# Moving dense-expert steps ahead of a recurrence, and splitting a run of exponentials, in a two-layer transformer kernel

## The reference

```
# x: [8, 512, 128]; xn = layernorm(x)
mixed = silu(causal_dwconv(zrms(xn) @ W_qkvz[:, :2048]))   # 16 blocks of 128 channels, 4 taps
q, k, v = split(mixed)                                     # 4 + 4 + 8 heads of 128; q and k normalised
g, beta = -exp(A_log) * softplus(a + dt_bias), sigmoid(b)  # per token and head
for t in tokens:                                           # the recurrence ("gated delta rule")
    S = S * exp(g[t]); delta = (v[t] - k[t] @ S) * beta[t]
    S = S + outer(k[t], delta); o[t] = q[t] @ S
core = rms(o) * gate_norm_w * silu(z);  h = xn + core @ W_out
attn = h + moe(zrms(h))                                    # 8 small experts, top 2
# the dense experts, on the same xn: every token goes through all 8
w = top2(softmax(xn @ w_router))                           # [tokens, 8], zero but for two
ffn = sum_e w[:, e] * (gelu(xn @ w1[e] + b1[e]) @ w2[e] + b2[e])     # 512 hidden channels each
x = x + attn + ffn
```

## Time and profile before

| | us |
|---|---|
| median of 3 runs | 2765.76 |
| lowest, highest | 2764.23, 2774.04 |
| the profiled execution | 2770.14 |
| its span, first to last instruction | 2768.3 |
| TensorE busy in it | 2453.1 (89%) |
| VectorE busy | 2028.8 (73%) |
| ScalarE busy | 1136.2 (41%) |
| GpSimd busy | 311.6 (11%) |

### The profile page before, as it was taken

How to read it: one execution, slowest core, us unless ns; L and a number is a source line. 1 busy time by engine, 2 the same in 40 slices (tenths; PEclk the granted TensorE clock), 3 DMA queues, 4 the chain that set the end, 5 groups by cost and what they waited for, 6 DMA issues and landing times.

```text
span 2768.3 us, 48745 instructions
## 1 busy us (share of the span) xinstructions
PE 2453.1 (89%) x15408; PEld 1596.9 (58%) x15408; DVE 2028.8 (73%) x6361; ACT 1136.2 (41%) x2066; POOL 311.6 (11%) x236
## 2 busy tenths in 40 slices
PE   2989888898989887899899899899899899899898
PEld 1434344443444444586586586586586586577576
DVE  4857676685867777768777867867867966966976
ACT  0132322313232234446446445445445445544544
POOL 1000000000000001121121110210210211211211
PEclk8988889898988987999999999999899999899999
DMA  5230413212130312201201201101101101211210
GB/s 157 78 93 24 108 37 88 55 62 72 46 103 25 105 43 66 69 5 58 70 4 59 62 9 62 54 17 62 47 25 62 47 25 36 66 32 32 62 39 31
DMA packets 158271, 152.01 MB, mean 55 GB/s; under 512 B 81128, under 2 KB 122672, under 8 KB 157520
## 3 DMA queue, kind: packets, MB, share of 16 engines
q1 hardware_dynamic: 155024, 142.83, 18.0%
q10 hardware_dynamic: 3008, 6.36, 0.6%
HBM read 121.29 MB, written 27.85 MB: 54 GB/s over the span
## 4 chain that ended last, share of the span: by engine, by line
PE 56%; DVE 25%; issue 12%; ACT 3%; DMA 2%; POOL 1%; SPq 1%; DVEq 0%; ACTq 0%; POOLq 0%
PE bank L910 5%; PE bank L922 5%; PE bank L580 4%; PE bank L592 4%; PE bank L583 4%; PE bank L608 3%; PE bank L502 3%; DVE arena L1605 3%; DVE arena L1663 3%; DVE arena L1661 3%; PE bank L648 3%; PE bank L897 2%; PE bank L879 2%; DVE arena L1617 2%; PE bank L870 2%
## 5 line engine op out<-in xcount | busy, mean ns | idle before, releaser
L922 PEld LDWEIGHTS bank<-wring,arena 128*128 128x128 f32 x2048 | 279.9, 202 | 136.4 <-issue 99.0
L1166 ACT ACTIVATE arena<-bank,w_b 128x512 f32<-128x512 f32 x256 | 175.1, 687 | 369.6 <-PE bank L910 369.3
L910 PE MATMUL bank<-arena,wring 128*128 128x512 f32 x512 | 295.0, 662 | 30.9 <-ACT arena L1166 30.9
L922 PE MATMUL bank<-wring,arena 128*128 128x128 f32 x2048 | 284.7, 287 | 22.8 <-DVE arena L1778 15.2
L1605 DVE SCALAR_TENSOR_TENSOR arena<-bank,w_convw,arena 128x511 f32<-128x511 f32 (+2 forms) x384 | 254.9, 737 | 11.6 <-ACT arena L1076 11.6
L1045 ACT ACTIVATE arena<-bank 128x512 f32<-128x512 f32 (+1 forms) x384 | 172.5, 534 | 186.9 <-PE bank L635 185.3
L1449 DVE CUSTOM_DVE_ANT_0 bank<-bank,arena 128x128 f32<-128x128 f32 (+3 forms) x512 | 249.2, 492 | 0.0
L1036 ACT ACTIVATE arena<-bank 128x512 f32<-128x512 f32 x128 | 76.5, 598 | 397.4 <-PE bank L580 397.4
L502 PE MATMUL bank<-w_ident,arena 128*128 128x128 f32 (+2 forms) x652 | 114.9, 303 | 84.5 <-DVE arena L1345 51.9
L592 PE MATMUL bank<-arena 128*128 128x128 f32 x1088 | 157.5, 288 | 2.7 <-DVE arena L1434 2.7
L580 PE MATMUL bank<-arena 128*128 128x512 f32 x256 | 148.7, 664 | 0.0
(11 more groups left out here) (284 smaller groups left out, 4845.8 us busy)
## 6 DMA issues: line engine op xcount, KB each, us to landing
wring<-in_w_last SPq DMA_DIRECT2D x66, 512.0 KB, 3.3
arena<-scrw SPq DMA_DIRECT2D x260, 128.0 KB, 3.0
arena<-scrg SPq DMA_DIRECT2D x32, 512.0 KB, 5.4
arena<-scrq SPq DMA_DIRECT2D x36, 192.0 KB, 3.8
arena<-scrk SPq DMA_DIRECT2D x36, 192.0 KB, 4.5
scrn<-arena SPq DMA_DIRECT2D x64, 64.0 KB, 1.9
arena<-scrn SPq DMA_DIRECT2D x8, 512.0 KB, 3.7
scrx<-arena SPq DMA_DIRECT2D x8, 512.0 KB, 3.5
```

Of the source, the lines that this page charges most:

```text
L910: mm(bank[HBANK[f]][:, :], wring[:, e % 2, k * P:(k + 1) * P], xn1T, start=True, stop=True).then_inc(*s["p_fh"].up)
L922: last = mm(bank[o][:, t * P:(t + 1) * P], GH[:, f % 2, t * P:(t + 1) * P], wring[:, e % 2, FC * P + k * D:FC * P + (k + 1) * D], start=(f ...
L1166: fn(GH[:, f % 2, :], bank[HBANK[f]][:, :], ACT.Gelu_apprx_tanh, bias=W["b1"][:, f:f + 1]).then_inc(*s["a_gh"].up)
```

## The change

The order of the steps is altered, and with it the banks. The decay step `gam` is split: four exponentials, then the copies of `qkv 10` and `gelu 2`, then the other four; `prep 1`, `prep 2` and `prep 3` come one dense step later each. `fh 8` goes to bank 1 like `fh 0` and stands ahead of `qkv 12`; `fh 9` and `fo 8` come ahead of `sub 0`. Twenty-four dense steps are now finished before the recurrence (22 before), and eight follow it (10 before). Each expert is one part in one bank, so there are eight `facc`. The first three experts are summed in bank 6, one after the other. `facc 1` is moved from between `sub 1` and `sub 2` to between `taps 12` and `taps 14`. The waits follow the banks.

```
-HBANK = (1,) + (7,) * 21 + (2,) * 10
-PARTS = ((0, 4, 6), (4, 8, 6), (8, 12, 2), (12, 16, 3), (16, 20, 6), (20, 22, 6), (22, 24, 3), (24, 28, 5), (28, 32, 3))
+HBANK = (1,) + (7,) * 7 + (1,) + (7,) * 15 + (2,) * 8
+OBANK = (6, 6, 6, 3, 2, 6, 5, 3)
...
-    order += [("fo", 5), ("gelu", 6), ("fh", 7), ("fo", 6), ("gelu", 7), ("taps", 10), ("silu", 8), ("qkv", 12), ("fo", 7), ("taps", 12)]
+    order += [("fo", 5), ("fh", 7), ("gelu", 7), ("fh", 8), ("fo", 6), ("gelu", 8), ("taps", 10), ("silu", 8), ("qkv", 12), ("fo", 7)]
+    order += [("taps", 12), ("facc", 1), ("silu", 10), ("qkv", 14), ("taps", 14), ("cz", 0), ("silu", 12), ("sz", 0), ("fh", 9), ("fo", 8), ("cz", 1)]
...
-    order += ffn(2) + [("nrm2", NT - 1, 0), ("nrm2", NT - 1, 1)] + ffn(1) + [("ct", NT - 1), ("facc", 6)] + ffn(1) + [("swo", NT - 1), ("h1",)] + ffn(3)
+    order += ffn(1) + [("nrm2", NT - 1, 0), ("nrm2", NT - 1, 1)] + ffn(1) + [("ct", NT - 1)] + ffn(1) + [("swo", NT - 1), ("h1",)] + ffn(2)
...
                 def cz(c):
+                    if c == 0:
+                        need("a_gh", 9)
...
-                        need(*(("a_inv", a0) if c else ("v_fo", 16)))
+                        need(*(("a_inv", a0) if c else ("v_fo", 20)))
...
                     if f == 1:
                         pe.wait_ge(*s["out_ready"].at(b, 0, late))
-                    elif f == 22:
+                    elif f == 24:
                         need("v_inv", INV_V * NT)
+                    elif f == 8:
+                        need("v_prep", 2 * NT)
                     elif f:
-                        need("a_gh", f)
+                        need("a_gh", f - (f == 9))
...
-                    if f == first and f:
-                        need(*(("v_fo", 4), ("a_sz", 3), ("a_sz", 4), ("v_fo", 8), ("v_fo", 20), ("v_inv", INV_V * NT), ("v_o", 2 * NT),
-                               ("v_fo", 28))[part - 1])
+                    if k == 0 and e:
+                        need(*(("v_fo", 4), ("v_fo", 8), ("a_sz", 4), ("a_sz", 3), ("v_fo", 12), ("v_o", 2 * NT),
+                               ("v_inv", INV_V * NT))[e - 1])
...
-                def gam():
-                    act.wait_ge(*s["v_gT"].at(b, 1, late))
-                    fn(eG.rearrange("p a b c -> p (a b c)"), bank[0][:, 0:96], ACT.Exp).then_inc(*s["a_eG"].up)
-                    for i in range(2 * NT):
+                def gam(half):
+                    if half == 0:
+                        act.wait_ge(*s["v_gT"].at(b, 1, late))
+                        fn(eG.rearrange("p a b c -> p (a b c)"), bank[0][:, 0:96], ACT.Exp).then_inc(*s["a_eG"].up)
+                    for i in range(NT * half, NT * half + NT):
                         act.wait_ge(*s["v_scan"].at(b, i + 1, late))
                         fn(Gam[:, i, :], Gam[:, i, :], ACT.Exp).then_inc(*s["a_gam"].up)
```

More of the change, by code:

```diff
@@ L846, in kt @@
                     if c < NT - 1:
[L847 removed]
+                        bk = after(*(("a_gh", 24), ("v_kd", 2), ("a_ct", 2))[c], 7)
                         for h in range(HK):
@@ L914, in ffn_out @@
                     e, k = f // FC, f % FC
-                    part = [f < end for _, end, _ in PARTS].index(True)
-                    first, end, o = PARTS[part]
                     pe.wait_ge(*s["a_gh"].at(b, f + 1, late))
-                    if f == first and f:
-                        need(*(("v_fo", 4), ("a_sz", 3), ("a_sz", 4), ("v_fo", 8), ("v_fo", 20), ("v_inv", INV_V * NT), ("v_o", 2 * NT),
-                               ("v_fo", 28))[part - 1])
+                    if k == 0 and e:
+                        need(*(("v_fo", 4), ("v_fo", 8), ("a_sz", 4), ("a_sz", 3), ("v_fo", 12), ("v_o", 2 * NT),
+                               ("v_inv", INV_V * NT))[e - 1])
                     for t in range(NT):
-                        last = mm(bank[o][:, t * P:(t + 1) * P], GH[:, f % 2, t * P:(t + 1) * P],
+                        last = mm(bank[OBANK[e]][:, t * P:(t + 1) * P], GH[:, f % 2, t * P:(t + 1) * P],
                                   wring[:, e % 2, FC * P + k * D:FC * P + (k + 1) * D],
-                                  start=(f == first and t == 0), stop=(f == end - 1), skip_group_check=True)
+                                  start=(k == 0 and t == 0), stop=(k == FC - 1), skip_group_check=True)
                     last.then_inc(*s["p_fo"].up)
```

39 lines of the change are left out of this document (17 added, 22 removed).

## The result

The changed kernel takes 2824.8 us (median of 4 runs, 2824.6 to 2829.6) against 2769.9 for the kernel before in the same comparison: ratio 1.0196, interval 1.0177 to 1.0216. It is slower by about 55 us. The forecast was 2799, so the sign was right, and the time lies 9 us above the range.

What follows compares the result with a forecast made beforehand. The recurrence starts at the later of two level lines, VectorE with its transfers and TensorE. +4.9 at the copy less 0.7 in the tail is +4.2 per pass, +34 over eight: 2804 profiled, 2799 median, range 2772 to 2816.

Steps and rivals of the forecast that it cites:

- What this is worth is when the last `prep` product is there ... I take 1.7: Decay phase: with the exponentials split, the last `prep` product ends 1.7 us earlier, at 1750.3 (gain 0 to 3.2).
- The wait for the weights: At `fh 8`, moved ahead of `qkv 12`: TensorE waits 4.4 us for the third expert's weights, landing at 1758.6.
- The clock behind it: From the landing, `fh 8` and `fo 6` take 1.9 to 3.8 us by the granted clock; 2.95 taken.
- TensorE's line: Dense steps ahead of the recurrence: 31.2 us again, ending at 1809.3, +3.7 against `inv 0 0` and later than VectorE's line.
- VectorE's line: Taps, `sub` and the transfers behind it: `sub` ends +2.85 us, and the line is ready for the recurrence at 1808.4.
- The recurrence: From its start on: ScalarE's copy for `inv 0 1` comes +4.9 us; no change in the recurrence's own length was priced.
- eight passes are alike: Second loop: its eight passes are alike, so a microsecond per pass is worth 8 in all.
- The tail: End of the pass, two dense steps less: `ct 3` gains nothing, `h2` gains 0.7 us (0 to 1.2).
- the weights are no wait: Rival at `fh 8`: weights land before TensorE needs them; -1.1 us per pass, 2757; chance 0.08.
- Absorbed: Rival: the wait is there but most is absorbed; +1 to +1.7 us per pass, 2774 to 2779; chance 0.13.
- Longer switches: Rival on ScalarE: each added function switch holds it another 1.28 us beyond its load; +6.8 per pass, 2820; chance 0.05.

Runs made afterwards that it cites:

- a_early: The changed kernel with SyncE issuing the third expert's weights between the two block transfers of the decays instead of behind all of them: 2791.9 us, ratio 1.0071.

## Why the prediction was right in sign and wrong in size

The steps, in us from the start of the pass; the forecast is built on the pass 1707.98, the measurement is the pass 1728.09 of the changed kernel.

| step | forecast | measured |
|---|---|---|
| last `prep` product ends | 42.3 | 44.8 |
| weights there, `fh 8` starts | 50.6 | 53.0 |
| `gelu 8` starts | 53.6 | 56.8 |
| `taps 12` starts | 57.3 | 60.5 |
| taps end | 66.4 | 69.5 |
| TensorE's dense steps end | 101.3 | 102.7 |
| `inv 0 0` starts | 101.3 | 103.3 |
| ScalarE's copy starts | 103.6 | 104.9 |
| first `swo` starts | 134.8 | 137.5 |
| pass ends | 215.7 | 218.4 |

**The step that failed: "What this is worth is when the last `prep` product is there ... I take 1.7".** It came 0.8 later than in that pass, not 1.7 earlier: 2.5 us per pass, 20 in all. The order does give the 1.7 (42.2, 18 times), when only 3.4 us at the lower clock fall there. I let `qkv 10` end at 1734.0, 26.0 into the pass, by the earlier trace rows, and hung `gelu 2`, and through it half of the exponentials, on that end. In the changed kernel it ends at 28.6 in each of passes 2 to 7, since the lower clock holds from 18.9 to 29.1. Before, those copies had VectorE's scans as cover and no exponential waited for them; the change took the cover away. The pass 1707.98 was also the wrong one to read: with passes 3 and 8 it has the earliest end of `qkv 10`, and passes 2, 5, 6 and 7 have it at 27.4 to 28.6. I used the stretches at 0.50 of the earlier trace rows at the wait for the weights alone.

**The wait for the weights** came as forecast: 3.98 us against 4.4, the landing 8.2 behind the product against 8.3. Since the transfer hangs on that product, the 2.5 us went through it undiminished.

**The clock behind it.** From landing to `gelu 8` it took 3.8 us, the upper end of 1.9 to 3.8; I took 2.95. That is 0.8 per pass. `gelu 8` to `taps 12` took 3.75, as forecast, and `facc 1` 1.12.

**TensorE's line** took 29.5 us from `fh 10` to the last `fo`, not 31.2. The 31.2 of the earlier trace rows held 3.4 us at the lower clock (from 1774.4), and I carried them over; in the changed kernel that stretch lies ahead of `fh 10`. So VectorE's line decided `inv 0 0`. The forecast had 0.9 us of room on that line (1808.4 against 1809.3), and the copy comes 1.7 behind `inv 0 0` instead of 2.3. That takes back part of the 3.2 us by which `taps 12` came later than forecast: 2.0 are left at `inv 0 0`, 1.3 at the copy.

**The recurrence** I took as unchanged, and in the mean it was: its first part takes 31.8 us before and 31.7 now. But I built on the pass 1707.98, which has no time at the lower clock there, where the changed kernel has 3.4 us in each of passes 2 to 8: +1.4 against that pass. The prediction's "eight passes are alike" was wrong; they take 209.7 to 215.0 us. The tail gave back 0.5 of the 0.7 against that pass: from the last `swo` to the pass's end it takes 36.6 us against 37.1, both with 10.2 us at the lower clock in it. In the mean it gave back nothing, 36.8 us in both kernels.

Per pass this makes 1.3 + 1.4 = 2.7, the difference between 215.7 and 218.4, some 21 us over eight passes: the profiled execution took 2824.7, and the sum against the profiled time was 2804. The other 4.4 to the forecast of 2799 I had taken off for the median, and the changed kernel's profiled time is at its median. Counted by means instead of by one pass, the forecast was +4.9 at ScalarE's copy and -0.7 behind, and it came to +6.7 at the copy and -0.3 behind.

Of the rivals, "the weights are no wait" was the right question: sent early, `taps 12` is 6.6 us earlier. But its price was wrong. It gave 2757 for weights in time, and a_early, which is just that, has 2791.9: `inv 0 0` is 0.7 later than before and the copy 1.9, where the rival had it 0.4 earlier. "Absorbed" is refuted by `inv 0 0` at +6.2 in the mean. "Longer switches" gave 2820, near the result, and is refuted by its rows: the table load at 1829.64 takes 1.28 and the silu follows 0.01 later, in the changed kernel too. The Trainium skill's figure for the drain in "ScalarE: Activation LUTs", "What ACT_TABLE_LOAD costs", is not seen here either. A time near the result was no proof of that mechanism.

What stays open: why passes 2 to 8 of the changed kernel all get the 10.2 us stretch around `qkv 10`, where two short fillers at the start of the recurrence, some 80 us later in the pass, are enough for four of seven passes to get a shorter one. The passes are linked, since a stretch of 10.2 us lies at their end as well, but no run here separates this. Fillers around `qkv 10` itself were not tried. That the clock of that stretch moves the last product rests on the 63 passes counted above, not on a run that changes it alone.

## What to carry to other kernels

Before a step is moved up to where an engine will wait for a transfer, find what issues the transfer and what that hangs on; if the transfer can go earlier, move it first. Price a new wait of TensorE by the wait and by what it does to the granted clock behind it, and read the kernel before over several passes, since one pass may be a lucky one. If parts of a change don't add up, lay the passes' means side by side, stretch by stretch: first see which engine's line comes last, then compare the same code at either clock. Useless matmuls in a wait are a good test, but a kernel that they make level with the old one does not prove that the clock was the loss, as long as the old one has not had the same fillers.
